# Two attention layers on one core: probabilities transposed in 64-row halves, scores in one float32 product, a staged start, and a new schedule

## The chip, the cores and the metric

The kernel runs on one core of a Trainium2 chip. The metric is the device time of one execution in microseconds (us), lower is better. The core has a matrix engine (TensorE, in the rows PE, and PEld for its weight loads), a vector engine (VectorE, DVE), a scalar engine (ScalarE, ACT), GpSimd (POOL) and a queue engine that issues the transfers (SyncE, SP). They run side by side and wait for each other through semaphores.

## The reference

The input is 16 sequences of 512 tokens of 128 features. Two blocks follow each other. Each normalises its input `xn`, then adds an attention and a feed-forward part:

```
x = x + _L0_attn_ref(xn, ...) + _L0_ffn_ref(xn, ...)      # 16 heads of 64, causal, distance penalty
xn = _layernorm(x)
x = x + _L1_attn_ref(xn, ...) + _L1_ffn_ref(xn, ...)      # 8 heads, each the difference of two softmaxes
# first attention, for each head:
sim = einsum('bhid,bhjd->bhij', q * SCALE, k) - |i - j| * slope, masked above the diagonal
out = softmax(sim) @ v
```

The second attention has 16 score maps (heads of 8 features, not causal). The feed-forward parts go from 128 to 512 features and back.

## The kernel before, in words

Every sequence is cut into 4 tiles of 128 tokens. The first attention is worked in 8 pairs of heads, the second in 16 score maps by groups of 4. There is one software pipeline: a body of 32 ticks (`TICKS`), four ticks to a pair, is written out 19 times (16 sequences and the overhang). In each body every engine has a fixed order of steps, written by hand and by tables: constants such as `LN0_AT`, `STACK_AT` or `KEY_LAG` say in which tick after a sequence's tick 0 a step stands. Numbers above 31 lie in the body of a later sequence, negative ones in that of an earlier one. So the first attention of one sequence (ticks 0 to 31 and a little more) shares a body with the second attention of an earlier one (ticks 58 to 86). Engines never reorder: what waits holds up all that stands behind it.

For one pair `p` of the first attention:

- TensorE projects q, k and v (L1304). ScalarE and VectorE together split q into `QH` and `QL`, and k into `KH` and `KL` (L795, L801, L1046, L1053): a rounded float32r part and its rest.
- `max_scores0` (L1364): for each of the four rows of 128 queries, three products `QH*KH + QL*KH + QH*KL` are summed in PSUM. The two heads stand in partitions 0 to 63 and 64 to 127, so each product is a pair of matmuls on half of the array's rows each. Row widths are 256, 256, 384 and 512 columns (at least 256).
- `row_max0` (VectorE, L1072) subtracts the distance term and takes the maximum; `exp0` (ScalarE, L827) takes the exponential and the row sums `lsum`; `invert_sums` (VectorE, L1079) takes the reciprocal of all 8 sums of a pair at once; `scale_probs` (GpSimd, L696) multiplies the 8 blocks of rows of `pq` by it, in place.
- `turn_probs` (TensorE, L1380) transposes the 20 blocks of 128x128 on and below the diagonal, in five groups that fill a PSUM tile of 512 columns each; `copy_turned` (ScalarE, L841) copies each tile to `pt`. `pv0` (L1392) multiplies by v, two heads side by side in 64 columns of the array each.

The second attention uses bf16 products for its maximum and its key scores (L1451, L1458; again two halves of rows), `pv1` (L1414; four quarters of 32 columns), and `stack`, which is SyncE's transfer of rotated queries and keys from a scratch tensor to `QS` and `KS` (L620), after `store_parts` (L610) has written them there.

All score and transpose tiles share five PSUM banks in turn (`score_order`, `SCB`): a tile may be written when the tile five places ahead of it has been read (`bank_free`). Projections and outputs share two more (`pj_order`).

Before the pipeline, 35 transfers bring in weights and tables (L568), all counted by one semaphore `s_ld`. VectorE, ScalarE and TensorE wait for all of them; then VectorE prepares the weights (21 small steps, `s_vprep`), and TensorE waits for that too.

## Time and profile before

| | us |
|---|---|
| median of 3 runs | 2792.95 (2787.28 to 2793.64) |
| the profiled execution, own time | 2788.22 |
| its span (first to last instruction) | 2786.4 |
| TensorE busy in the span | 2554.3 (92%) |
| VectorE, ScalarE, GpSimd busy | 1927.8 (69%), 1962.1 (70%), 1398.8 (50%) |
| mean granted TensorE clock, as a share of 2.4 GHz | 0.98 |

Between the profiled execution's own time and its span lie 1.8 us. Busy shares are averages over three stages: a start without matmuls, a long middle in which all sequences look alike, and an end in which only the second attention of the last sequence is left. A matmul's row shows its length with the latency; what one costs in a stream is the distance from one start to the next. The float32 matmuls stand in the trace as two matmuls each.

### The profile page before, as it was taken

The numbers are of one execution on the slowest core, as the hardware profiler recorded it, in microseconds if no ns is written. First come the engines' busy times: TensorE is split into PE (matmuls) and PEld (weight loads), VectorE is DVE, ScalarE is ACT, GpSimd is POOL, SyncE is SP. The second block draws the span as 40 slices with busy tenths as digits, with TensorE's granted clock in tenths as the row PEclk, the third lists the DMA queues.
The fourth block names the chain that finished last, engine by engine and source line by source line (L and its number), as shares of the span: only waits on it lengthen the run. The fifth ranks groups of instructions, "written<-read, shape, count | busy, mean of one in ns | idle before, by whom it ended". The sixth has DMA issues, their size and how long they took to land.

```text
span 2786.4 us, 49789 instructions
## 1 busy us (share of the span) xinstructions
PE 2554.3 (92%) x16640; PEld 1389.1 (50%) x16640; DVE 1927.8 (69%) x5381; ACT 1962.1 (70%) x4707; POOL 1398.8 (50%) x1353
## 2 busy tenths in 40 slices
PE   3788999999999999999999999999999999999867
PEld 1455555555555545555554555555455555554421
DVE  3336777677777767777776867767676776867664
ACT  2566777777777677787777868777787777778434
POOL 3556455463645546364554636456464645646211
PEclk9899999999999999999999999999999999999976
DMA  2002001020200102020010202002020200202020
GB/s 86 4 1 50 2 17 39 5 50 5 46 5 17 39 6 50 5 47 5 15 41 5 51 1 51 5 10 46 5 50 2 50 5 6 50 2 50 1 50 5
DMA packets 59822, 68.39 MB, mean 25 GB/s; under 512 B 11056, under 2 KB 55344, under 8 KB 56368
## 3 DMA queue, kind: packets, MB, share of 16 engines
q1 hardware_dynamic: 59568, 65.21, 10.3%
q8 instruction: 135, 2.21, 0.3%
q14 instruction: 119, 0.97, 0.1%
HBM read 35.04 MB, written 29.36 MB: 23 GB/s over the span
## 4 chain that ended last, share of the span: by engine, by line
PE 75%; DVE 11%; ACT 5%; issue 5%; POOL 3%; SPq 1%; DMA 0%; DVEq 0%; POOLq 0%; ACTq 0%
PE pj L1304 18%; PE sc L1364 10%; PE pj L1392 10%; PE op L1414 9%; PE sc L1380 9%; PE sc L1458 5%; PE pj L1404 4%; PE pj L1319 4%; PE sc L1451 4%; DVE pq L1072 4%; POOL pq L696 2%; DVE mx L1125 2%; ACT pt L862 2%; PE pj L1296 2%; ACT oraw L846 1%
## 5 line engine op out<-in xcount | busy, mean ns | idle before, releaser
L696 POOL TENSOR_SCALAR pq<-pq,rsum 128x128 f32<-128x128 f32 (+3 forms) x1024 | 1103.0, 1096 | 989.6 <-DVE rsum L1079 989.0
L1125 DVE TENSOR_REDUCE mx<-sc 128x1 f32<-128x512 f32 x1024 | 649.5, 681 | 213.4 <-PE sc L1458 213.2
L862 ACT ACTIVATE pt<-sc 128x512 f32<-128x512 f32 x1024 | 551.3, 601 | 213.0 <-PE sc L1451 210.8
L1072 DVE CUSTOM_DVE_ANT_0 pq<-sc,relkey 128x128 f32<-128x128 f32 (+3 forms) x1024 | 457.1, 483 | 249.2 <-PE sc L1364 242.5
L841 ACT ACTIVATE pt<-sc 128x512 f32<-128x512 f32 x640 | 381.7, 600 | 275.6 <-PE sc L1380 274.1
L827 ACT ACTIVATE pq<-pq,mx 128x128 f32<-128x128 f32 (+3 forms) x1024 | 569.0, 568 | 3.0 <-DVE mx L1072 3.0
L1380 PE MATMUL sc<-ident,pq 128*128 128x128 f32 x2560 | 395.3, 283 | 40.0 <-POOL pq L696 26.9
L1380 PEld LDWEIGHTS sc<-ident,pq 128*128 128x128 f32 x2560 | 288.9, 142 | 222.3 <-issue 130.9
L1392 PE MATMUL pj<-pt,v 128*64 128x512 f32 (+3 forms) x2048 | 303.9, 438 | 14.7 <-DVE KL L1053 13.0
L1414 PE MATMUL op<-pt,v 128*32 128x512 f32 x2048 | 282.6, 626 | 6.4 <-ACT pt L862 6.2
L1304 PE MATMUL pj<-xnT,wqkv 128*128 128x512 f32 x512 | 284.9, 640 | 0.8 <-ACT xnT L772 0.8
L1458 PE MATMUL sc<-KS,QS 48*128 48x512 bf16 x1024 | 246.0, 392 | 35.4 <-DVE mx L1072 18.1
L1364 PE MATMUL sc<-KH,QH 64*128 64x256 f32 (+2 forms) x1024 | 207.9, 399 | 22.2 <-ACT pt L862 14.1
L1392 PEld LDWEIGHTS pj<-pt,v 128*64 128x64 f32 x2048 | 141.8, 136 | 173.0 <-issue 130.6
L1451 PE MATMUL sc<-QS,KS 51*128 51x512 bf16 x1024 | 211.2, 398 | 18.1 <-ACT pt L862 7.8
L827 ACT ACTIVATION_READ_ACCUMULATOR pq<-pq,mx 128x1 f32 x1024 | 211.5, 206 | 0.0
L1364 PEld LDWEIGHTS sc<-KH,QH 64*128 64x128 f32 x1024 | 99.1, 184 | 213.4 <-issue 176.2
L1364 PE MATMUL sc<-KH,QL 64*128 64x256 f32 (+2 forms) x1024 | 168.9, 320 | 0.0
L1364 PE MATMUL sc<-KL,QH 64*128 64x256 f32 (+2 forms) x1024 | 168.8, 319 | 0.0
L1451 PEld LDWEIGHTS sc<-QS,KS 51*128 51x128 bf16 x1024 | 49.9, 93 | 213.2 <-issue 136.1
L818 ACT ACTIVATE att<-pj 128x512 f32<-128x512 f32 x128 | 76.4, 597 | 99.1 <-PE pj L1392 97.1
L1304 PE MATMUL pj<-wqkv,xnT 128*128 128x128 f32 x1024 | 145.3, 285 | 0.4 <-ACT y L789 0.4
(107 smaller groups left out, 3335.0 us busy)
## 6 DMA issues: line engine op xcount, KB each, us to landing
scr_p<-y SPq DMA_DIRECT2D x160, 128.0 KB, 2.4
QS<-scr_p SPq DMA_DIRECT2D x32, 384.0 KB, 5.8
KS<-scr_p SPq DMA_DIRECT2D x32, 384.0 KB, 8.8
x_in<-in_L_attn_x SPq DMA_DIRECT2D x16, 256.0 KB, 2.9
scr_p<-tanh SPq DMA_DIRECT2D x32, 128.0 KB, 2.4
out_x<-xres SPq DMA_DIRECT2D x16, 256.0 KB, 2.3
QS<-nrow SPq DMA_DIRECT2D x192, 4.0 KB
wqkv<-in_L_attn_w_qkv SPq DMA_DIRECT2D x1, 1536.0 KB, 8.4
```

The lines of the kernel that those rows point to most:

```text
L696: pool.tensor_scalar(rows, rows, rsum[:, p % NROWS, c:c + 1], None, ALU.mult).then_inc(s_scl, 1)
L827: act.activation(rows, rows, ACT.Exp, scale=-1.0, bias=mx0[:, p % NROWS, c:c + 1], accum_out=lsum[:, p % NROWS, c:c + 1]).then_inc(s_exp0, 1)
L841: act.activation(pt[:, base:base + T], sc[tile_bank("tr0", m)][:, :], ACT.Copy).then_inc(s_ev, 1)
L862: act.activation(pt1[:, GS * (m % 2) + 2 * j + h, :], sc[tile_bank("st1", 2 * n + h)][:, :], ACT.Exp, scale=float(DS) ** -0.25).then_inc(s ...
L1072: dve.tensor_tensor_reduce(out=pq[:, at:at + width], in0=sc[tile_bank("mx0", m)][:, left:left + width], in1=relkey[:, T - width:T], scale= ...
L1125: dve.reduce_max(mx1[:, g % 2, at:at + 1], sc[tile_bank("mx1", 2 * t + h)][:, :], AXIS.X).then_inc(s_mxd1, 1)
L1304: last = pe.matmul(t[:, c * k:c * (k + 1)], w(k), x(k), start=True, stop=True)
L1364: last = pe.matmul(sc[tile_bank("mx0", m + j)][:, left:left + width], x[r, b, P * row:P * (row + 1)], y_[r, b, 0:width], start=c == 0, sto ...
L1380: last = pe.transpose(t[:, to:to + P], pq[:, at:at + P], ident[:, :])
L1392: last = pe.matmul(t[DH * j:DH * (j + 1), P * k:T], v0[:, p % NBUF, k, DH * j:DH * (j + 1)], pt[:, base:base + WIDTH[k]], start=k == 0, st ...
L1414: last = pe.matmul(op[32 * j:32 * (j + 1), :], v1[:, k, (GS * g + j) // 2, :], pt1[:, GS * (k % 2) + j, :], start=k == 0, stop=k == NT - 1)
L1458: pe.matmul(sc[tile_bank("mx1", 2 * t + h)][:, :], QS[r, slot, P * q:P * (q + 1)], KS[r, slot, :], start=True, stop=True).then_inc(s_mxf1, 1)
```

## The change

It has five parts.

1. `turn_probs`: each block is transposed as two halves of 64 rows (`h`), which go to two PSUM tiles, in three groups (8, 8 and 4 blocks) instead of five. The copy of `copy_turned` puts the halves side by side again: six copies per pair, four of 512 and two of 256 columns.
2. `max_scores0`: one float32 product of `Q0` and `K0` instead of the three float32r ones. The rows are 128, 256, 384 and 512 columns wide. ScalarE copies q, VectorE copies k; the splitting steps are gone.
3. `invert_sums` and `scale_probs` work in four steps `q` of two sums each; the first two steps stand one pair earlier than before.
4. The loads come in three groups with a semaphore each; the first x is the first transfer of all. What prepares weights stands in ticks 1, 10 and 14 of the first body, and each first user waits for its group only.
5. Schedule: other ticks, `KEY_LAG` 14 instead of 13, another order of the steps in each tick.

```diff
-TURNED = (((0, 0),), ((1, 0),), ((0, 1), (0, 3)), ((1, 1), (1, 3)), ((0, 2), (1, 2)))
+TURNED = (((0, 0), (1, 0)), ((0, 1), (0, 3), (1, 1), (1, 3)), ((0, 2), (1, 2)))
-STACK_AT = (54, 57)
+STACK_AT = (47, 50)
-KEY_LAG = 13
+KEY_LAG = 14
@@ sync
-                for dst, src in loads:
-                    sp.dma_start(dst, src).then_inc(s_ld, 16)
+                sp.dma_start(x_in[:, :, :], x_v[0]).then_inc(s_x, 16)
+                for n in range(3):
+                    for dst, src in loads[n]:
+                        sp.dma_start(dst, src).then_inc(s_ld[n], 16)
@@ vector
-            def split_q(i, p):
-            def split_k(i, p):
+            def copy_k(i, p):
+
+                b, u = pj_use(i, f"k{p}")
+                dve.wait_ge(s_pjf[b], u)
+                dve.tensor_copy(K0[:, p % NQ, :], pj[b][:, :]).then_inc(s_pje[b], 1)
-                dve.wait_ge(s_exp0, i.upto(L0N, 8 * p + 8))
-                dve.reciprocal(rsum[:, p % NROWS, :], lsum[:, p % NROWS, :]).then_inc(s_rc, 1)
+                dve.wait_ge(s_exp0, i.upto(L0N, 8 * p + 2 * q + 2))
+                dve.reciprocal(rsum[:, p % NROWS, 2 * q:2 * q + 2], lsum[:, p % NROWS, 2 * q:2 * q + 2]).then_inc(s_rc, 1)
@@ tensor
-            pe.wait_ge(s_ld, NLOAD)
-            pe.wait_ge(s_pset, N_PSET)
-            pe.wait_ge(s_vprep, N_VPREP)
-            pe.wait_ge(s_aprep, N_APREP)
+            pe.wait_ge(s_ld[0], NLOAD[0])
-                    width = max(P * (row + 1), 2 * P)
-                    for c, (x, y_) in enumerate(((QH, KH), (QL, KH), (QH, KL))):
-                        for j in range(2):
+                    width = P * (row + 1)
+                    for j in range(2):
+                        last = pe.matmul(sc[tile_bank("mx0", m + j)][:, left:left + width], Q0[r, b, P * row:P * (row + 1)],
+                                         K0[r, b, 0:width], start=True, stop=True)
-                        last = pe.transpose(t[:, to:to + P], pq[:, at:at + P], ident[:, :])
+                    for h in range(2):
+                        r = slice(HALF * h, HALF * (h + 1))
+                        last = pe.transpose(sc[tile_bank("tr0", m + h)][:, HALF * n:HALF * (n + 1)], pq[r, at:at + P], ident[r, r])
@@ scalar, copy_turned
-                act.activation(pt[:, base:base + T], sc[tile_bank("tr0", m)][:, :], ACT.Copy).then_inc(s_ev, 1)
+                act.activation(to[:, :, h, :], sc[tile_bank("tr0", m)][:, 0:cols].rearrange("p (n c) -> p n c", c=HALF),
+                               ACT.Copy).then_inc(s_ev, 1)
```

TensorE, in the middle of the program, the last tick of one pair and the first of the next, before (`ident,pq` are the transposes, `KH`/`QH` and the like the scores, `QS,KS` the second attention, `xnT` projections):

```order
L1380 MATMUL sc<-ident,pq 128x128 x4
L1451 MATMUL sc<-QS,KS 128x512 x2
L1380 MATMUL sc<-ident,pq 128x128 x4
L1304 MATMUL pj<-xnT,wqkv 128x512
L1380 MATMUL sc<-ident,pq 128x128 x4
L1451 MATMUL sc<-QS,KS 128x512 x2
L1304 MATMUL pj<-xnT,wqkv 128x512
L1364 MATMUL sc<-KH,QH 128x256 x2
L1364 MATMUL sc<-KH,QL 128x256 x2
L1364 MATMUL sc<-KL,QH 128x256 x2
```

The same place of the changed program:

```order
L1492 MATMUL sc<-KS,QS 128x512 x2
L1411 MATMUL sc<-ident,pq 128x64 x16
L1448 MATMUL op<-pt,v 32x512 x4
L1485 MATMUL sc<-QS,KS 128x512 x2
L1492 MATMUL sc<-KS,QS 128x512 x2
L1332 MATMUL pj<-xnT,wqkv 128x512
L1485 MATMUL sc<-QS,KS 128x512 x2
L1492 MATMUL sc<-KS,QS 128x512 x2
L1332 MATMUL pj<-xnT,wqkv 128x512
L1394 MATMUL sc<-K,Q 128x128 x2
L1394 MATMUL sc<-K,Q 128x256 x2
L1411 MATMUL sc<-ident,pq 128x64 x24
```

The transposes stand in two runs of 16 and 24 halves per pair instead of five groups of 4, and next to other matmuls that use half of the array's rows. Over one whole body (the rows from one sequence to the next) TensorE changes between whole array, row halves, column halves and column quarters 138 times before and 123 times after.

GpSimd, in the middle of the program, before (`rsum` rows scale the probabilities, the others are small norms):

```order
L696 TENSOR_SCALAR pq<-pq,rsum 128x128
L696 TENSOR_SCALAR pq<-pq,rsum 128x256
L696 TENSOR_SCALAR pq<-pq,rsum 128x128
L696 TENSOR_SCALAR pq<-pq,rsum 128x256
L668 TENSOR_SCALAR veps<-mv 128x4
L670 TENSOR_TENSOR rstd<-veps,minus_half 128x4
L696 TENSOR_SCALAR pq<-pq,rsum 128x384 x2
L696 TENSOR_SCALAR pq<-pq,rsum 128x512 x2
```

After:

```order
L713 TENSOR_SCALAR pq<-pq,rsum 128x384 x2
L681 TENSOR_SCALAR veps<-mv 128x4
L683 TENSOR_TENSOR rstd<-veps,minus_half 128x4
L713 TENSOR_SCALAR pq<-pq,rsum 128x512 x2
L713 TENSOR_SCALAR pq<-pq,rsum 128x128
L713 TENSOR_SCALAR pq<-pq,rsum 128x256
L721 TENSOR_SCALAR mse<-ms 128x8
L723 TENSOR_TENSOR rms<-mse,minus_half 128x8
```

The rows are the same, but each step of two now waits only for its own two sums, and the small row blocks of the next pair follow the large ones of this pair.

SyncE, the transfers of one sequence in the middle of the program, before:

```order
L610 DMA scr_p<-y 16x8x512 x5
L610 DMA scr_p<-tanh 16x8x512
L610 DMA scr_p<-y 16x8x512 x5
L610 DMA scr_p<-tanh 16x8x512
L620 DMA QS<-scr_p 48x4096 x2
L620 DMA KS<-scr_p 48x4096 x2
L595 DMA out_x<-xres 128x4x128
```

After:

```order
L620 DMA scr_p<-y 16x8x512 x5
L620 DMA scr_p<-tanh 16x8x512
L632 DMA QS<-scr_p 48x4096 x2
L620 DMA scr_p<-y 16x8x512 x5
L620 DMA scr_p<-tanh 16x8x512
L632 DMA KS<-scr_p 48x4096 x2
L605 DMA out_x<-xres 128x4x128
```

The query stack, which waits until the key scores of the sequence before are all done, now stands in front of the stores of the key parts.

## Rows read from the trace of the kernel before

**Rows 1.** Windows: us, busy PE, PEld, DVE, ACT, POOL (x), clock, DMA, GB/s

```profile
50.00:152.50 102.50, 76.74 (x469) 48.63 (x469) 42.82 (x161) 63.10 (x169) 56.88 (x54) 0.91 0.01 4
...
1426.80:1590.00 163.20, 156.62 (x1042) 85.85 (x1041) 120.09 (x336) 122.22 (x294) 86.87 (x84) 1.00 0.11 24
2549.30:2786.40 237.10, 181.28 (x966) 73.55 (x964) 137.39 (x309) 110.97 (x229) 45.65 (x46) 0.81 0.09 20
```

**Rows 2.** Waits of PE, 500 to 2300 us: total us, times, longest

```profile
PE pj L1392 <- DVE KL L1053: 8.4, 12, 0.7
PE pj L1304 <- DVE KL L1053: 7.1, 11, 0.9
```

**Rows 3.** Waits of PE, 50 to 200 us

```profile
PE sc L1380 <- POOL pq L696: 22.5, 6, 5.1
```

**Rows 4.** Timeline of PE: start us, length us, instructions (transposes, then a projection)

```profile
1406.06 1.04 PE L1380 MATMUL sc<-ident,pq 128*128 128x128 f32 x8
1406.93 1.02 PE L1304 MATMUL pj<-xnT,wqkv 128*128 128x512 f32 x2
```

**Rows 5.** Groups by form: PE weight loads and one score matmul (mean ns last before the second bar)

```profile
L1380 PEld LDWEIGHTS sc<-ident,pq 128*128 128x128 f32 x2560 | 288.9, 142 | 222.3 <-issue 130.9 <-POOL pq L696 31.3 <-ACT pt L841 19.6
...
L1392 PEld LDWEIGHTS pj<-pt,v 128*64 128x64 f32 x2048 | 141.8, 136 | 173.0 <-issue 130.6 <-ACT pt L841 16.8
...
L1304 PEld LDWEIGHTS pj<-wqkv,xnT 128*128 128x128 f32 x1024 | 124.1, 191 | 24.1 <-issue 18.6 <-ACT y L789 4.8 <-ACT xnT L772 0.3
...
L1364 PE MATMUL sc<-KH,QL 64*128 64x256 f32 x512 | 73.9, 278 | 0.0
```

**Rows 6.** Timeline of PE: float32r scores of rows 0 and 1, and of row 3

```profile
1403.72 0.51 PE L1364 MATMUL sc<-KH,QH 64*128 64x512 f32 x2
...
1404.62 1.16 PE L1304 MATMUL pj<-w_l,xnT 128*128 128x128 f32 x8
...
1409.33 0.38 PE L1364 MATMUL sc<-KH,QH 64*128 64x256 f32 x2
1409.52 0.31 PE L1364 MATMUL sc<-KH,QL 64*128 64x256 f32 x2
...
1410.00 0.31 PE L1364 MATMUL sc<-KL,QH 64*128 64x256 f32 x2
1410.24 0.66 PE L1380 MATMUL sc<-ident,pq 128*128 128x128 f32 x4
```

**Rows 7.** Timeline of PE: transposes, values by two heads, scores of row 2

```profile
1413.33 0.60 PE L1380 MATMUL sc<-ident,pq 128*128 128x128 f32 x4
1413.86 2.37 PE L1392 MATMUL pj<-pt,v 128*64 128x512 f32 x16
1416.17 1.13 PE L1304 MATMUL pj<-xnT,w 128*128 128x512 f32 x2
...
1417.66 0.44 PE L1364 MATMUL sc<-KH,QH 64*128 64x384 f32 x2
...
1418.29 0.40 PE L1458 MATMUL sc<-KS,QS 48*128 48x512 bf16 x2
```

**Rows 8.** Groups by form: the splitting steps and the copy of a turned tile

```profile
L841 ACT ACTIVATE pt<-sc 128x512 f32<-128x512 f32 x640 | 381.7, 600 | 275.6 <-PE sc L1380 274.1
...
L1046 DVE SCALAR_TENSOR_TENSOR QL<-pj,qscale,QH 128x512 fp32r<-128x512 f32 x128 | 94.8, 740 | 50.3 <-ACT QH L795 50.3
...
L801 ACT ACTIVATE KH<-pj 128x512 fp32r<-128x512 f32 x128 | 77.0, 601 | 1.2 <-PE pj L1304 1.2
```

**Rows 9.** Timeline of PE: the first matmul of the program

```profile
39.39 1.09 PE L1296 MATMUL pj<-ident,xn 128*128 128x128 f32 x4 [39.39 <-DVE xn L1024]
```

**Rows 10.** DMA issues: KB each, median us from issue to landing

```profile
scr_p<-y SPq DMA_DIRECT2D x160, 128.0 KB, 2.4
...
KS<-scr_p SPq DMA_DIRECT2D x32, 384.0 KB, 8.8
...
wqkv<-in_L_attn_w_qkv SPq DMA_DIRECT2D x1, 1536.0 KB, 8.4
```

**Rows 11.** Timeline of SyncE: the stack of the keys is issued

```profile
1402.54 0.77 SPq L620 DMA_DIRECT2D KS<-scr_p  x2
```

More of the change, by code:

```diff
@@ L222, in pj_order @@
             order += misc
+        elif r == 1:
+            second(n, 0)
             order.append(("pv", *pair_at(s, 3)))
-        elif r == 1:
+            order += misc
+            second(n, 1)
+        elif r == 2:
+            second(n, 0)
+            order.append(("v", *pair_at(s, -1)))
+            order += misc
+            second(n, 1)
+        else:
             second(n, 0)
@@ L259, in turned @@
         p, ago = pair_at(s, lag)
-        order.append(("tr0", ago, 5 * p + g))
+        order.extend(("tr0", ago, 6 * p + 2 * g + h) for h in range(2))
     for n in range(TICKS):
@@ L307, in ago, with first @@
         return Seq(self.lo - d, self.j)
+    def first(self):
+        return self.j is None and self.lo == 0
     def live(self):
@@ L574, in load_x @@
             def load_x(i):
[L576 to L577 removed]
+                if i.first():
                     return
@@ L730, in body @@
                     s, r = divmod(n, 4)
+                    if b.first() and n == 0:
+                        clear()
                     if r == 0:
@@ L749, in body @@
                             scale_probs(i, p, 3)
+                    elif r == 2:
+                        p, i = b.pair(s, 0)
+                        if i is not None:
+                            scale_probs(i, p, 0)
                         small(b, n)
+                    else:
+                        small(b, n)
+                        p, i = b.pair(s, 0)
+                        if i is not None:
+                            scale_probs(i, p, 1)
             pipeline(pool, body)
@@ L909, in body @@
                     s, r = divmod(n, 4)
+                    if b.first():
+                        prepare(n)
                     if r == 0:
+                        p, i = b.pair(s, -1)
+                        if i is not None:
+                            copy_q(i, p)
                         second_attention(b, n, 0)
```

468 lines of the change are left out of this document (227 added, 241 removed).

## The prediction

> **What bounds the kernel now.** I looked at windows first. One sequence of the middle, from the first projection of its head pairs to that of the next, takes 163.2 us; TensorE is busy for 156.6 of it, ScalarE for 122.2, VectorE for 120.1, GpSimd for 86.9, all at the full clock (granted 1.00, the level of 2.4 GHz) [rows 1]. Thirteen such periods lie between 285.6 and 2405.3 us, 163.05 us each. So three quarters of the program is TensorE's stream, and what it spends there counts thirteen times. The waits of TensorE in the middle are small: the two largest that the change touches are for the last part of the split keys, 8.4 and 7.1 us over 1800 us, or eleven sequences [rows 2]. The start is another matter: the first matmul begins at 39.4 us [rows 9], and in the first pairs TensorE is busy for 76.7 of 102.5 us [rows 1], with 22.5 us of waits for GpSimd's scaling of the probabilities [rows 3]. The end, 237 us with 181 us of TensorE work, holds the second attention of the last sequence alone [rows 1].
>
> **Transposes.** Eight transposes of 128x128 start at 1406.06, the next step at 1406.93: 0.109 us each [rows 4], 20 per pair, 2.18 us. A half has 64 columns to stream instead of 128, and the two halves use different rows of the array, as the two heads of the scores do now. From the streaming alone a pair of halves would cost 0.055 us. Two other bounds are near. The weights (128 columns) must come in: a load of 64 columns lasts 136 ns, of 128 columns 191, so 0.86 ns per column on about 81 ns of latency; the transposes' own loads last 142 ns [rows 5], so about 61 ns without the latency. And two instructions of each kind must be issued: two score matmuls of 0.278 us [rows 5] cover 0.31 us together [rows 6], so the second starts 0.03 us after the first, and two such steps make 0.06 to 0.07. I take 0.066. From above the nearest row is the float32r pair, 0.12 us per pair of 256 columns [rows 6]; that is the bound if it is the pair and not the columns that costs. Sum: 8 pairs x 20 x (0.066 - 0.109) = **-6.9 us per sequence**; upper end +1.8.
>
> **Scores.** Before: rows 0 and 1 take 0.91 us (1409.33 to 1410.24), row 3 0.90 (1403.72 to 1404.62) [rows 6], row 2 0.63 (1417.66 to 1418.29) [rows 7]; 2.44 us. After, each head streams 128 + 256 + 384 + 512 columns in float32. That is exactly what the values step does: sixteen matmuls, two heads side by side, 1413.86 to 1416.17, 2.31 us [rows 7]. It divides columns of the array and not rows, but float32r rows go side by side as well [rows 6]. With two more entries of about 0.17 us (three groups instead of one; their drain and first load, below) it is 2.65: **+0.2 us per pair, +1.6 per sequence**. If float32 halves did not run together it would be twice the streaming, +2.1 us more per pair.
>
> **Changes of the array's division.** Four transposes from 1413.33 need 0.44, yet the values step begins 0.53 later [rows 7]; between whole-array steps nothing is lost (1406.93 above is 8 x 0.109) [rows 4]. After the scores, the next transposes start 0.24 after a last pair that needs 0.12 [rows 6]. So a change costs 0.10 us, and 0.05 to 0.11 more where the first weights can't be loaded ahead. The order has 138 changes per sequence before and 123 after: 15 x 0.15 = **-2.3 us**. The Trainium skill (TensorEngine Tiling, Key Properties) says that changing the tiling mode drains the engine; these rows agree, 0.10 us each.
>
> **Projections and copies.** K is ready after one copy instead of a ScalarE step and a VectorE step. The waits for it are (8.4 + 7.1) / 11 = **-1.4 us per sequence** [rows 2]. ScalarE loses a step of 0.60 us and gains one copy: six instead of five, two of them half as wide, about +0.2 us, from copies of 0.60 [rows 8]. VectorE loses 0.74 [rows 8] and one like it, gains a copy of about 0.6 and three more reciprocals of some 0.2 us. Both engines end a little lighter than 122 and 120 us per sequence, against 155 of TensorE; if TensorE did not cover them, these edits would still be gains.
>
> **Waits that come.** A faster TensorE meets the readers of its five PSUM banks earlier, and now writes four banks of transposes in a row, which ScalarE empties in 2 x 0.6 + 2 x 0.4 = 2.0 us while TensorE has values steps to do. I put **+1.0 us per sequence** on this, from nothing up to 5. Sum for the middle: -6.9 + 1.6 - 2.3 - 1.4 + 1.0 = -8.0, so 155 us per sequence, x 13 = **-104 us**.
>
> **The start.** Before, everything waits for all 35 transfers and then for the preparation. After, x is first, and TensorE needs eight transfers more; the largest of them lands 8.4 us after its issue [rows 10]. Issues take about 0.4 us each (two in 0.77) [rows 11], so it goes out third, at about 1.7 us, and the group is there at 10 to 12 us, and the norms of x, which need only the first transfer, fit under it. First matmul at about 12 instead of 39.4 [rows 9]: **-27 us**, of which I keep it all, since the preparation for tick 1 (about 3 us of VectorE) moves into a stage that has room.
>
> **The first pairs.** GpSimd starts when all eight sums are inverted and TensorE waits 22.5 us for it [rows 3]. After, half of the blocks are scaled before the last exponential, and I expect most of this to go, some 17 us, plus the cheaper transposes of 15 pairs, 8 us: **-25 us**. **The end:** the last sequence's eight pairs keep the same gain, **-7 us**; the 237 us behind them have neither transposes of this kind nor such scores, 0.
>
> **Sum:** 2788.2 - 104 - 27 - 25 - 7 = 2625 for a profiled execution; its own time was 4.7 us under the median of the three runs, so **2630 us**.
>
> **The rivals.**
> *Halves as dear as wholes.* A pair of halves costs 0.12 us, as a float32r pair does [rows 6], from issue or weight loads. Then the middle has +1.8 instead of -6.9 and TensorE is no faster, so no new waits come: about 0 per sequence, and the start and first pairs remain (-27 and -18): 2748 us. For it: no row shows a pair under 0.11 us. Against: 191 versus 142 ns of the loads, and the 0.03 us step. The Trainium skill (TensorE: Matmul & The Clock Gate, LDWEIGHTS) gives a load as columns / 1.2 ns whatever the number of rows, 107 ns here; by that rule the halves save nothing, and the same page (Wait, 56 ns, not 53.3 ns?) gives 62 ns per matmul if the instructions are decoded in software, 124 for a pair.
> *New waits.* The five banks, or the stack. The key stack is issued at 1402.5 [rows 11] and lands 8.8 us later [rows 10], 1411.3; the first score of the new sequence starts at 1418.3 [rows 7], 7 us of slack. After, the key parts are stored only behind the query stack: six issues of 0.4 us and more and a landing of 2.4 us [rows 10] come in between, 3 to 5 us in all, and the sequence is 8 us shorter on the way; 2 to 4 us are left. If either costs 4 us per sequence more: 2630 + 13 x 4 = 2682.
> *Float32 halves one after another (the other side).* If the two heads' float32 matmuls don't share the array, the scores take 2.1 us more per pair, 17 us per sequence: 2630 + 16 x 17 = 2900 us. It decides from 10 us per sequence on. For it: no row has float32 on row halves. Against: the values step has its sixteen matmuls in 2.31 us [rows 7], which is the time of eight.
> *The start doesn't gain.* Were the first group as late as the whole, 27 us would be missing, 2657; inside the range.
>
> **How the numbers follow.** Forecast 0.57; halves as dear 0.16; new waits 0.19; one after another 0.08. 2630 is the first. Its own range is 2590 to 2665. The range 2580 to 2750 takes in the second and third and leaves out the fourth. A measurement here tells 0.3% (8 us) from no change. Faster: the first three except 0.03 of the second, where waits would add to it, 0.89; within 0.3% 0.03; slower 0.08.
>
> **What would show it.** The distance from one pair of half transposes to the next (0.066); the length of a middle period (155); scores of row 3 at about 0.43 us per float32 pass of both heads; the first matmul at 12 us; the waits for GpSimd in the first 150 us under 6; TensorE's waits for ScalarE's copies and for `QS`, `KS`. I would be wrong if pairs of halves stand 0.11 us or more apart, if the second head's matmuls start when the first head's end, or if TensorE's idle share in a middle period rises above the 4% of now by more than 2%.

## The result, and the profile after

The changed kernel takes 2723.15 us (median of 4 runs, 2718.66 to 2727.31), the kernel before 2793.3 beside it (2787.28 to 2796.29): ratio 0.9751, 95% interval 0.9726 to 0.9776. It is faster by 70 us, where 163 were forecast. The time is inside the range, the sign is right, and the size is not: more than half of the gain is missing. (The two profiled executions show less, 60.9 us between their spans: the one before ran 5 us under its median, this one 4 us over its own.) Where the gain is missing, the windows tell. The changed kernel's, with the columns of [rows 1] (the first two sequences, one of the middle, and the stretch behind the last projections):

```profile
16.60:121.90 105.30, 84.32 (x537) 45.69 (x537) 47.15 (x196) 62.09 (x173) 59.63 (x58) 0.89 0.09 27
121.90:241.20 119.30, 107.28 (x825) 62.22 (x823) 64.27 (x247) 83.26 (x223) 80.95 (x77) 0.99 0.13 30
1377.40:1539.70 162.30, 150.93 (x1138) 75.81 (x1136) 116.51 (x353) 118.18 (x295) 87.78 (x84) 1.00 0.10 24
2496.50:2725.50 229.00, 176.57 (x1022) 69.54 (x1021) 138.25 (x315) 109.82 (x232) 44.20 (x44) 0.85 0.09 22
```

I cut both programs at the same step, ScalarE's copy of the first q of a sequence, and compared the pieces (us):

| piece | before | after | difference | forecast |
|---|---|---|---|---|
| up to the first copy of q | 43.4 | 16.6 | -26.8 | -27 |
| sequences 0 and 1 | 109.2 + 133.1 | 105.3 + 119.3 | -17.7 | -25 |
| 13 sequences of the middle | 13 x 163.05 | 13 x 162.34 | -9.3 | -104 |
| last sequence and end | 381.1 | 373.9 | -7.2 | -7 |
| span | 2786.4 | 2725.5 | -60.9 | -163 |

The start came out as forecast, and the first pairs fell 7 us short. The end agrees in number only. Cut once more, at the last copy of q, its first part holds all but the tail of the last sequence's eight pairs, before and after:

```profile
2405.30:2549.30 144.00, 139.08 (x940) 75.83 (x939) 103.58 (x281) 106.86 (x260) 72.74 (x70) 1.00 0.08 19
```

```profile
2351.60:2496.50 144.90, 134.62 (x1023) 67.31 (x1022) 101.27 (x298) 103.37 (x260) 76.78 (x73) 1.00 0.08 18
```

They gained nothing (144.0, then 144.9), and from there to the last transposes it is 54.9, then 55.8 us. The 8 us came in the stretch behind them, where none had been forecast: 237.1 us at a granted clock of 0.81 [rows 1], 229.0 at 0.85. Most of them lie between the last transposes and the last output projection, before and after:

```profile
2604.20:2641.60 37.40, 31.65 (x197) 12.99 (x199) 24.05 (x49) 19.21 (x38) 1.86 (x2) 0.91 0.01 2
```

```profile
2552.30:2582.40 30.10, 26.64 (x182) 10.15 (x178) 20.15 (x40) 16.93 (x35) 1.86 (x2) 1.00 0.01 2
```

Both the order (15 matmuls fewer fall into it) and the clock differ there, and no run parts the two. The length of the whole stretch goes with the clock in kernels of the changed order too: 234.0 us at 0.82 in e11, 225.0 at 0.87 in e3, 223.2 at 0.88 in e7.

The middle missed most: a period is 0.7 us shorter and not 8. Yet TensorE does have less to do in it, 150.9 us of 162.3 where it had 156.6 of 163.2 [rows 1]. Its idle part rose from 6.6 to 11.4 us (4% to 7%). So the work went, and idle time came in its place.

The work went as forecast. In the timeline of TensorE (start us, length us), the float32 scores of row 3 with the key scores behind them, and a run of twelve pairs of halves:

```profile
1406.32 1.13 PE L1394 MATMUL sc<-K,Q 64*128 64x512 f32 x4
1407.28 0.38 PE L1485 MATMUL sc<-QS,KS 51*128 51x512 bf16 x2
...
1418.63 0.97 PE L1411 MATMUL sc<-ident,pq 64*128 64x64 f32 x24
```

The twelve pairs start between 1418.631 and 1419.369: the last ones follow each other every 0.0625 us, and the two of a pair 3 to 4 ns apart (7 to 11 ns in the run of sixteen below). Of row 3, the first pass of both heads starts at 1406.32, the second at 1406.85, and the key score at 1407.28: the heads share the array in float32 too.

What came is in TensorE's waits over eleven sequences (403.5 to 2188.9 us; total us, times, longest):

```profile
PE sc L1411 <- DVE mx L1095: 38.1, 77, 1.0
PE sc L1492 <- DVE mx L1095: 15.8, 52, 0.5
PE sc L1394 <- ACT pt L885: 8.9, 22, 0.6
PE sc L1492 <- ACT pt L863: 8.1, 22, 0.4
```

L1411 is a transpose, L1095 VectorE's pass over a score tile that takes the row maxima; 38.1 / 11 is 3.5 us per sequence, in seven waits of half a microsecond. The kernel before, over eleven sequences (448.8 to 2242.1 us), had 4.2 there, and nearly as much as now at the maximum scores (L1458, now L1492):

```profile
PE sc L1458 <- DVE mx L1072: 14.3, 56, 0.5
PE sc L1380 <- DVE mx L1072: 4.2, 11, 1.0
```

All listed waits together rose from 63.5 to 118.2 us, 5.0 per sequence. Those for VectorE's row maxima are 3.1 of it (19.3 to 53.9 us). The waits for K gave 1.4 back. The other 3.2 are many small ones of 0.3 to 0.8 us per sequence, most of them new, for copies and sums that empty other banks (L813, L836, L863, L1069, L1116, L1148); no run tests these.

Its waits for KL [rows 2] are gone, and none for K stands in the changed kernel's list. One of the seven, in the changed kernel's timeline of all engines:

```profile
1396.14 0.93 PE L1394 MATMUL sc<-K,Q 64*128 64x128 f32 x8
...
1396.90 0.66 PE L1411 MATMUL sc<-ident,pq 64*128 64x64 f32 x16
1397.21 0.29 DVE L1095 CUSTOM_DVE_ANT_0 pq<-sc,relkey 128x128 f32<-128x128 f32 x1 [0.73 <-PE sc L1394]
...
1397.42 0.42 DVE L1095 CUSTOM_DVE_ANT_0 pq<-sc,relkey 128x256 f32<-128x256 f32 x1
...
1397.77 0.69 DVE L1076 COPY K<-pj 128x512 f32<-128x512 f32 x1
...
1398.00 0.46 PE L1411 MATMUL sc<-ident,pq 64*128 64x64 f32 x8 [0.44 <-DVE mx L1095]
```

TensorE writes the two score tiles of rows 0 and 1, then sixteen half transposes into two more banks, then wants two banks for the last eight. (One score tile belongs to each of the two heads.) With five banks in rotation the second of these is the bank of the first score tile, five tiles back. VectorE starts when the scores are done, reads the tile twice and is through at 1397.85. Sixteen halves take TensorE only half a microsecond, and it stands until 1398.00. It is VectorE that waited first (0.73 us for the scores), so no engine is overloaded here: it is a round trip with too little work beside it. (A round trip: TensorE writes a tile, VectorE reads it, and only then may TensorE write its bank again.)

### The profile page after: what moved, and what is told of

Read it like the earlier page. It is cut to its first block, busy times and chain, and to the rows that moved or that the text cites. A ratio compares the mean times of both kernels' runs of the same rounds, so it can differ in the third digit from the quotient of the medians.

```text
span 2725.5 us, 52475 instructions
## 1 busy us (share of the span) xinstructions
PE 2468.1 (91%) x18176; PEld 1232.3 (45%) x18176; DVE 1869.4 (69%) x5637; ACT 1896.9 (70%) x4707; POOL 1411.5 (52%) x1353
## 4 chain that ended last, share of the span: by engine, by line
PE 65%; DVE 14%; ACT 9%; issue 3%; DMA 0%; SPq 0%; POOLq 0%; DVEq 0%; ACTq 0%; POOL 0%
PE pj L1332 16%; PE sc L1394 10%; PE pj L1424 9%; PE op L1448 8%; PE sc L1492 5%; DVE pq L1095 5%; PE pj L1350 4%; PE pj L1438 4%; ACT pt L885 4%; PE sc L1411 4%; PE sc L1485 3%; DVE mx L1148 2%; PE pj L1324 2%; ACT pt L863 1%; ACT pq L845 1%
## 5 line engine op out<-in xcount | busy, mean ns | idle before, releaser
L1148 DVE TENSOR_REDUCE mx<-sc 128x1 f32<-128x512 f32 x1024 | 653.3, 684 | 334.3 <-PE sc L1492 331.3
L885 ACT ACTIVATE pt<-sc 128x512 f32<-128x512 f32 x1024 | 558.4, 608 | 220.2 <-PE sc L1485 219.7
L1095 DVE CUSTOM_DVE_ANT_0 pq<-sc,relkey 128x128 f32<-128x128 f32 (+3 forms) x1024 | 459.0, 486 | 315.5 <-PE sc L1394 308.3
L863 ACT ACTIVATE pt<-sc 128x512 f32<-128x512 f32 (+1 forms) x768 | 353.8, 530 | 186.9 <-PE sc L1411 185.9
L1394 PE MATMUL sc<-K,Q 64*128 64x128 f32 (+3 forms) x2048 | 383.0, 471 | 25.0 <-ACT pt L885 11.2
L1411 PE MATMUL sc<-ident,pq 64*128 64x64 f32 x5120 | 233.6, 228 | 69.0 <-DVE mx L1095 58.4
L1492 PE MATMUL sc<-KS,QS 48*128 48x512 bf16 x1024 | 243.7, 387 | 47.5 <-DVE mx L1095 20.4
L1411 PEld LDWEIGHTS sc<-ident,pq 64*128 64x128 f32 x5120 | 201.0, 140 | 177.4 <-issue 134.2
L1394 PEld LDWEIGHTS sc<-K,Q 64*128 64x128 f32 x2048 | 147.0, 187 | 252.3 <-issue 158.2
L1492 PEld LDWEIGHTS sc<-KS,QS 48*128 48x128 bf16 x1024 | 60.8, 94 | 196.3 <-DVE mx L1095 64.7
L1332 PEld LDWEIGHTS pj<-wqkv,xnT 128*128 128x128 f32 x1024 | 125.8, 193 | 39.7 <-issue 25.7
L811 ACT ACTIVATE tanh<-pj,b1h 128x512 f32<-128x512 f32 x128 | 88.3, 690 | 75.4 <-PE pj L1332 70.4
```

The source lines that it names most:

```text
L863: act.activation(to[:, :, h, :], sc[tile_bank("tr0", m)][:, 0:cols].rearrange("p (n c) -> p n c", c=HALF), ACT.Copy).then_inc(s_ev, 1)
L885: act.activation(pt1[:, GS * (m % 2) + 2 * j + h, :], sc[tile_bank("st1", 2 * n + h)][:, :], ACT.Exp, scale=float(DS) ** -0.25).then_inc(s ...
L1095: dve.tensor_tensor_reduce(out=pq[:, at:at + width], in0=sc[tile_bank("mx0", m)][:, left:left + width], in1=relkey[:, T - width:T], scale= ...
L1148: dve.reduce_max(mx1[:, g % 2, at:at + 1], sc[tile_bank("mx1", 2 * t + h)][:, :], AXIS.X).then_inc(s_mxd1, 1)
L1332: last = pe.matmul(t[:, c * k:c * (k + 1)], w(k), x(k), start=True, stop=True)
L1394: last = pe.matmul(sc[tile_bank("mx0", m + j)][:, left:left + width], Q0[r, b, P * row:P * (row + 1)], K0[r, b, 0:width], start=True, stop ...
```

## The experiments

The first theory (A): the middle is bound by such round trips. Work taken from TensorE beside one turns into waiting, and comes back as time only in part. Its rivals: (B) TensorE's work is what bounds, so the halves' gain was eaten by something that costs work; (C) VectorE's and ScalarE's work as a whole sets the period; and theories on single terms. All ratios are to the kernel before, measured on the same chip.

**e1: whole blocks in the changed order.** Banks and order as changed; each bank gets whole blocks, and ScalarE's copies, as many and as long (0.60 and 0.40 us), write them without the interleaving. (A line `...` in a cut of code stands for lines left out.)

```diff
+                half = len(blocks) // 2
...
-                    for h in range(2):
-                        r = slice(HALF * h, HALF * (h + 1))
-                        last = pe.transpose(sc[tile_bank("tr0", m + h)][:, HALF * n:HALF * (n + 1)], pq[r, at:at + P], ident[r, r])
...
+                    h, c = divmod(n, half)
+                    last = pe.transpose(sc[tile_bank("tr0", m + h)][:, P * c:P * (c + 1)], pq[:, at:at + P], ident[:, :])
```

> The changed kernel, but each block is transposed whole (one matmul of 128 columns instead of two halves of 64); same groups, tiles, copies and order. In the trace of the changed kernel a pair of halves takes 0.0625 us, a whole block took 0.109, so this adds 160 x 0.047 = 7.4 us of TensorE work per sequence. Theory A (the transposes' gain is real but was turned into waits for PSUM banks, above all the 0.6 us between the 16 and the 8 transposes of a tick, which ends when VectorE has read the scores): the added work partly fills those waits, a period of 162.3 grows to 164 to 167, in all +30 to +75 us, near 2775. Theory B (TensorE's work is the bound, and the lost time is somewhere else): +7.4 us per period, +118 us, near 2840. Theory C (the halves gain nothing at all): 2723.

Measured: 2752.81 us, ratio 0.9859 (0.9844 to 0.9873); period 164.6. In one period (columns as above):

```profile
401.00:565.50 164.50, 156.32 (x977) 80.39 (x976) 116.31 (x352) 117.98 (x295) 87.98 (x84) 1.00 0.10 24
```

The waits of the transposes for VectorE, in 403.5 to 2188.9 us, fell from 38.1 us to

```profile
PE sc L1411 <- DVE mx L1095: 6.8, 22, 0.3
```

TensorE has 5.4 us more to do than with halves and the period is 2.2 us longer; its idle part falls from 11.4 to 8.2. So 7.4 us of transposes by start-to-start distances (160 pairs of halves, 0.109 less 0.0625) are worth 2.2 us. Theory B (2840) falls; A had put the time too high as well (2775).

**e2: one pass for the scores.** Q and K as float32r, one product per tile, rows 256 columns wide at least (so the scores are coarser): a cut of TensorE's work in another place.

```diff
-        Q0 = sb("Q0", [P, NQ, T])
-        K0 = sb("K0", [P, NQ, T])
+        Q0 = sb("Q0", [P, NQ, T], F32R)
+        K0 = sb("K0", [P, NQ, T], F32R)
...
-                    width = P * (row + 1)
-                    left = P if row == 1 else 0
+                    width = max(P * (row + 1), 2 * P)
+                    left = 2 * P if row == 1 else 0
```

> The changed kernel with q and k rounded to float32r and their product taken in one pass (rows of at least 256 columns); the rounding error of the scores stays in, so the output is coarser. TensorE work falls by about 1.5 us per pair, 12 us per sequence (4 passes of 1280 columns against one pass of 1408). Theory B, TensorE's work is the bound: a period of about 150, some 190 us less in all, near 2535. Theory A, waits for banks and for the row maxima are as much of the bound as work: the scores are ready earlier too, so row maxima move forward with them, and half to two thirds of the 12 us come through: a period of 154 to 156, near 2610. If the period stays within 2 us of 162.3, TensorE's work in the scores is not on the path at all.

Measured: 2645.63 us, 0.9471 (0.9457 to 0.9485); period 157.15, in which about 5 us came back of the 12 that had been put on the cut. That is less than either forecast (B 2535, A 2610 with a period of 154 to 156). Part of it is the clock, which had stood at 1.00 in the middle of the changed kernel and does not here. Two sequences:

```profile
394.10:552.90 158.80, 143.74 (x1074) 73.85 (x1073) 116.58 (x352) 117.57 (x296) 88.49 (x84) 0.98 0.10 25
1180.50:1336.30 155.80, 140.99 (x1075) 71.74 (x1074) 116.49 (x352) 117.62 (x296) 88.56 (x84) 1.00 0.11 25
```

At 1.00 TensorE is busy for 9.9 us less than in the changed kernel, and the period is 6.5 us shorter. This is inside A's range: two thirds of the busy time came back, half of the 12. The waits for L1095 grew to 46.0 us at the transposes and 34.7 at the maximum scores (in 403.5 to 2188.9 us).

**e3: one group of loads.** x first as changed, all other transfers in one group that everything waits for.

```diff
+        loads = [loads[0] + loads[1] + loads[2]]
+        s_ld = [s_ld[0]] * 3
+        NLOAD = [16 * len(loads[0])] * 3
```

> The changed kernel, but all 35 loads are counted by one semaphore again and every first user waits for all of them (x is still the first transfer; what prepares weights stays in the first body). It undoes the staged start alone. The last load landed near 27 us before, the first group lands near 10 us now: the first projection should come about 16 us later, and the whole 14 to 18 us, near 2739. If the start's gain were only that the preparation left the path, the time would move by less than 5 us.

Measured: 2739.57 us, 0.9809 (0.9789 to 0.983). The first copy of q is at 34.1 us instead of 16.6, the period stays at 162.4: of the 26.8 us, the groups are worth 17.5 and x first with the later preparation the rest.

**e4: the second run of transposes later.** On TensorE alone, behind the small transposes, the feed-forward steps and a values step of its tick; no bank changes its place in the rotation.

```diff
-                        p, i = b.pair(s, 2)
-                        if i is not None:
-                            turn_probs(i, p, 2)
                         second_turns(b, n, 0)
                         second_turns(b, n, 1)
                         others(b, n)
                         second_values(b, n, 1)
+                        p, i = b.pair(s, 2)
+                        if i is not None:
+                            turn_probs(i, p, 2)
```

> The changed kernel, but the second run of transposes (4 blocks, two tiles) in the first tick of a pair stands behind the other steps and the values step of that tick instead of right behind the first run. No tile or bank changes its place in the turn order, only TensorE's order. Theory A says that 0.6 us per pair of waiting between the two runs (4.9 us per sequence) is time in which that other work can be done: where there is some (perhaps half of the pairs) the wait goes, 2 to 3 us per sequence, 35 us in all, near 2688. Theory B: no change, 2723. A loss would mean that ScalarE's copies of these tiles, now later, hold the next tick.

Measured: 2704.12 us, 0.9689 (0.9673 to 0.9706), 19 us faster than the changed kernel, and their intervals don't meet. Period 161.3, and sequences 0 and 1 7.7 us shorter (they scatter by a few us from kernel to kernel, below). The waits in 403.5 to 2188.9 us:

```profile
PE sc L1492 <- DVE mx L1095: 22.9, 65, 0.6
PE sc L1411 <- DVE mx L1095: 15.0, 45, 0.4
...
PE pj L1424 <- DVE y L1116: 8.8, 11, 0.8
...
PE pj L1332 <- DVE K L1076: 5.5, 11, 0.5
```

The transposes wait 23 us less, the three others here 18 us more and three further ones 11 less. Of these 17 us, 11 x 1.1 = 12 come back.

**e5, e6: VectorE's order.** In e5 the row maxima of the second score tile stand directly behind those of the first, ahead of the norms and of the copy of K; in e6 with the edit of e4 too.

```diff
                             row_max0(i, p, 0)
+                            row_max0(i, p, 1)
                         norms(b, n)
                         p, i = b.pair(s, -1)
                         if i is not None:
                             copy_k(i, p)
-                        p, i = b.pair(s, 0)
-                        if i is not None:
-                            row_max0(i, p, 1)
```

> The changed kernel with one change of VectorE's order: in the first tick of a pair the second pair of row maxima (row 2 of the scores; rows 0 and 1 are the first) follows directly on the first, ahead of the normalization steps and of the copy of the next pair's K (the copy takes about 0.66 us). Theory A, that the second run of half transposes waits about 0.6 us eight times a sequence because VectorE reads its bank late, behind the copy of K: most of the 38.1 us that TensorE waits at the transposes for row maxima in eleven sequences goes, the period falls from 162.3 to 158.5 to 160 us, time 2680 to 2700. Theory B, that TensorE waits there for something that merely comes late with the whole of VectorE's and ScalarE's work: the wait moves to another line, period 162 to 163, time 2718 to 2728.

Measured: 2730.43 us, 0.9769 (0.9751 to 0.9788), period 162.7; the waits of the transposes, in the same stretch:

```profile
PE sc L1409 <- DVE mx L1095: 40.2, 77, 1.2
```

Nothing was cured, though the length of the wait (put at 0.6; 0.5 in the rows) and of the copy of K (0.69) had looked alike. The tile that the edit moves ahead holds the second head's rows 0 and 1, not row 2 as the expectation has it. I had blamed the wrong tile: the copy stands behind the read that TensorE waits for, as the timeline above shows once the banks are counted: TensorE goes on with the last eight halves at 1398.00, in the middle of the copy (1397.77 to 1398.46).

> Both edits together: row maxima next to each other on VectorE, and the second run of transposes behind the other work of its tick on TensorE (alone 2704). Theory A, that the two cure the same wait: about what the better of the two gives, with at most 10 us on top, 2675 to 2700. Theory B, that the late run's gain came from other waits than VectorE's order: the two add up, or the new order only shifts the wait and the time stays at 2704.

Measured: 2718.59 us, 0.9737 (0.9724 to 0.9751), period 162.2: 14 us worse than e4 alone. The copy of K is now what is late; e4 had 5.5 us of this wait of a projection:

```profile
PE pj L1330 <- DVE K L1076: 18.6, 22, 1.2
```

**e7: sums inverted and blocks scaled at once,** in the second tick of the next pair (VectorE and GpSimd).

```diff
...
-                            invert_sums(i, p, 3)
+                            for q in range(4):
+                                invert_sums(i, p, q)
...
```

> The changed kernel with the row sums of a pair inverted and the blocks scaled all in the second tick of the next pair, as they stood nearly in the kernel before, in place of four steps. Theory A, that the four steps help where few pairs are in flight and change nothing in the middle: the first two sequences give back some 5 to 10 us of the 17.7 that they gained, the period stays within 0.5 us of 162.3, time 2728 to 2735. Theory B, that GpSimd's scaling in four steps keeps the middle going too: period 163 to 165, time 2740 to 2765. Theory C, that the extra small instructions on VectorE cost the middle something: period 161 to 162, time 2710 to 2720.

Measured: 2747.58 us, 0.9844 (0.983 to 0.9857). The period is unchanged (162.3), sequences 0 and 1 take 126.8 + 129.6 us, 31.8 more than in the changed kernel, and the end is 6 us shorter, at a granted clock of 0.88 in its last stretch where the changed kernel had 0.85. In 50 to 200 us:

```profile
PE sc L1395 <- POOL pq L713: 26.0, 7, 5.7
```

The changed kernel has 6.8 us of this there, the one before 22.5 [rows 3]. So the program is 24 us slower, all from the start, more than twice what A gave to the steps. Not all of the 31.8 us is waiting. The two sequences:

```profile
16.10:142.80 126.70, 90.33 (x537) 49.36 (x537) 47.77 (x194) 62.43 (x172) 60.26 (x56) 0.86 0.08 22
142.80:272.50 129.70, 111.43 (x826) 64.22 (x824) 65.60 (x247) 83.46 (x222) 80.79 (x76) 0.95 0.12 27
```

The same matmuls keep TensorE busy for 201.8 us at 0.86 and 0.95, and for 191.6 at 0.89 and 0.99 in the changed kernel. These 10 us go with the lower clock.

**e8: float32 scores alone, in the kernel before.** One product of copied Q and K instead of three of split ones.

```diff
-                    for c, (x, y_) in enumerate(((QH, KH), (QL, KH), (QH, KL))):
+                    for c, (x, y_) in enumerate(((Q0, K0),)):
```

> The kernel before with one part of the change alone: scores of the first attention from one float32 product, Q and K copied once each (by ScalarE and by VectorE), no splitting; transposes in whole blocks, order and loads as before. By the terms on record, +1.6 us of TensorE work and -1.4 us of waits for KL a sequence: 2795, no change. By the traces of the two kernels, where the scores' columns rose from 14.9 to 17.7 us a sequence (+2.8) and the waits go: +1.4 a sequence, 2815. Theory C, that ScalarE and VectorE, each freed of some 5 us of copies a sequence, come earlier with everything else: 2760 to 2785.

Measured: 2804.34 us against 2791.16, 1.0042 (1.003 to 1.0055): slower. The period is 164.35 (+1.3), and in it:

```profile
449.40:613.70 164.30, 158.08 (x978) 80.93 (x977) 114.84 (x328) 118.54 (x287) 86.91 (x84) 1.00 0.11 24
```

TensorE's work is 1.5 us more, as forecast (+1.6). The waits for K did not go (403.5 to 2188.9 us; there had been 8.4 and 7.1 us for KL [rows 2]):

```profile
PE pj L1384 <- DVE K L1046: 11.5, 22, 0.9
...
PE pj L1296 <- DVE K L1046: 7.1, 11, 0.6
```

TensorE's two waiting steps, the values of the pair and a projection, read no K: they want the bank of K's projection, which VectorE's step is the last to read. That step stands where it stood, behind the row maxima, which would be why one step instead of two frees the bank no sooner. And 5 us of work less on VectorE and 4 less on ScalarE gave nothing; theory C falls here.

**e9: one more read of the first score tile,** 256 columns into a buffer that nobody reads, before the read that frees the tile.

```diff
+                    if c == 1:
+                        dve.tensor_tensor_reduce(out=twice[:, 0:width], in0=sc[tile_bank("mx0", m)][:, left:left + width],
+                                                 in1=relkey[:, T - width:T], scale=-SLOPES[2 * p + j], scalar=-MASKED,
+                                                 op0=ALU.add, op1=ALU.min, accum_out=twice_mx[:, 0:1])
```

> The changed kernel with one more read by VectorE of the score tile of rows 0 and 1 (128x256, into a buffer that nobody reads; 0.35 us, eight a sequence), just before the read that gives the tile free. Theory A, that the second run of half transposes waits for exactly this tile (with five banks in rotation it takes the bank of the first score tile of its tick, and VectorE's two reads of it end after the first run): the period rises by nearly eight times 0.35 us, +2.3 to +2.9 us, time 2753 to 2762. Theory B, that the wait at the transposes stands for something that is late anyway: period within 0.5 us of 162.3, time 2718 to 2730.

Measured: 2759.47 us, 0.9874 (0.9861 to 0.9888); period 164.8, +2.4 for eight reads, 0.30 us of each 0.35. The waits of the transposes (402.5 to 2215.1 us):

```profile
PE sc L1417 <- DVE mx L1101: 61.6, 77, 1.4
```

38.1 has become 61.6, 2.1 us per sequence. VectorE is busy for 119.2 of 164.7 us meanwhile, so it is not its load: this one read is on the path in nearly every pair. Theory A's mechanism is shown, and the tile is the right one. What it doesn't show is that the period would shrink by as much without the wait; e10 asks that.

**e10, e11: the first run of transposes ahead of the scores,** on TensorE, in the rotation and in ScalarE's copies; then no transpose wants VectorE's tile. e11 has the edit of e4 too.

```diff
+            turned(s, 2, 1)
             second(n, 0)
             tops(s, 0, 0)
-            turned(s, 2, 1)
             turned(s, 2, 2)
```

> The changed kernel with the first run of half transposes (sixteen) moved ahead of the score tiles of its tick on TensorE, and ScalarE's copies of it moved ahead of its exponentials; the second run then takes a bank that ScalarE and not VectorE gives free, and the score tile is read while other products run. Theory A, that the price is the chain score tile, VectorE's read, transposes: the 38.1 us of waits for row maxima at the transposes go below 10, the period falls to 158 to 160.5, time 2670 to 2700. Theory B, that in order issue only moves the wait to another tile of the five banks (ScalarE's copies late): period 161 to 163, time 2705 to 2730. Theory C, that exponentials and scores, half a microsecond later in their tick, delay the row maxima of the second attention: period over 163, time over 2735.

Measured: 2731.13 us, 0.9781 (0.9766 to 0.9795), period 161.7. The wait at the transposes fell from 38.1 to 3.0 us; in its place (411.6 to 2190.5 us):

```profile
PE sc L1490 <- DVE mx L1093: 21.4, 66, 0.4
PE sc L1490 <- ACT pt L863: 13.3, 44, 0.3
PE pj L1422 <- DVE y L1114: 12.0, 11, 1.1
PE pj L1422 <- DVE K L1074: 10.8, 22, 0.7
...
PE sc L1409 <- DVE mx L1093: 3.0, 11, 0.3
```

3.2 us of waits per sequence went, and the period fell by 0.6. The first two sequences took 9.1 us more, which outweighs it. That is theory B of this run (whose 2730 it misses by 1 us): the wait moves, here above all to the values step (L1422), which needs a bank that VectorE empties late. The new order moves ScalarE's and TensorE's other steps too, so the run doesn't price the one wait alone.

> As the run before, with the second run of transposes also behind the other work of its tick (which alone gave 2704). Theory A: 2660 to 2690, a little under the run before it, as the two waits are parts of one. Theory B: 2700 to 2715.

Measured: 2743.99 us, 0.9816 (0.9801 to 0.9831), period 162.3. What helped alone (e4) costs 13 us here, and both theories (2660 to 2690, 2700 to 2715) are wrong; no run says why.

**e12: float32r scores in the changed kernel.** Splits on ScalarE and VectorE and three products, all else as changed.

```diff
-                        last = pe.matmul(sc[tile_bank("mx0", m + j)][:, left:left + width], Q0[r, b, P * row:P * (row + 1)],
-                                         K0[r, b, 0:width], start=True, stop=True)
...
+                            last = pe.matmul(sc[tile_bank("mx0", m + j)][:, left:left + width], x[r, b, P * row:P * (row + 1)],
+                                             y_[r, b, 0:width], start=c == 0, stop=c == 2)
```

> The changed kernel with the scores of the first attention as before: Q and K split into a high and a low part by ScalarE and VectorE, three float32r products a tile at the old places of the splits; half transposes, order and loads as in the changed kernel. In the kernel before the float32 scores alone cost 13 us (2804 against 2791). Theory A, that they cost the same here: 2708 to 2715. Theory B, that in the changed order, with ScalarE and VectorE nearer to TensorE's path, the splits' two further instructions a pair cost more than the columns save: 2735 to 2760. Terms on record: the float32 scores are worth 0.2 to 1.2 us a sequence less work than waits, so 2720 to 2740.

Measured: 2743.27 us, 0.9817 (0.9803 to 0.983), period 163.9 although TensorE has 1.3 us less to do in it:

```profile
406.00:569.40 163.40, 149.60 (x1202) 80.10 (x1200) 122.97 (x360) 121.63 (x304) 87.89 (x84) 1.00 0.10 24
```

The waits for the row maxima (L1115) at the transposes grew from 38.1 us:

```profile
PE sc L1435 <- DVE mx L1115: 46.8, 66, 1.8
```

So the two splitting steps more per pair seem to lengthen the round trip. But 163.9 is a mean of two kinds of sequences. Some take 163.1 to 163.5 us, mostly at clock 1.00 as above, the others 164.2 to 164.4 at 0.99, such as

```profile
1388.60:1553.00 164.40, 151.22 (x1202) 80.23 (x1200) 122.83 (x360) 121.68 (x304) 87.38 (x84) 0.99 0.10 24
```

Float32 scores cost 1.3 us a sequence in the old kernel. In the new one they are worth 0.8 to 1.1 at equal clock, and 1.6 with the lower clock of this run. Their price is not a property of theirs.

## Why the prediction was wrong

Of the kernel before, e8, e1 and the changed kernel, each adds to the one ahead: float32 scores; then, all at once, the new order and banks with loads and steps; then halves.

| | period | TensorE busy | idle |
|---|---|---|---|
| before | 163.05 | 156.6 | 6.6 |
| + float32 scores (e8) | 164.35 | 158.1 | 6.2 |
| + order, banks, early steps (e1) | 164.6 | 156.3 | 8.2 |
| + halves (the changed kernel) | 162.3 | 150.9 | 11.4 |

(Busy and idle are of one period each, at clock 1.00.) The step that failed is **"Waits that come"**, +1.0 us per sequence with 5 as the upper end. Term by term:

- *Transposes*, -6.9: the pair takes 0.0625 us where 0.066 were taken, so the work is 7.4 us less. Right, and the rival "halves as dear as wholes" is false. The prediction weighed the Trainium skill (TensorE: Matmul & The Clock Gate, LDWEIGHTS), by which a load would take 107 ns whatever the rows; here each half of the rows takes a new load of 128 columns every 62.5 ns, so the trace does not agree with that for this form. Of 7.4 us, 2.2 reached the period (e1).
- *Scores*, +1.6: e8 measured +1.5 of TensorE's work and +1.3 of the period. Right. The rival "one after another" is false.
- *Changes of the array's division*, -2.3: e1 differs from e8 by order and banks, and has 1.8 us less work and 2.0 more idle. The gain may well be in the work; none of it reached the period.
- *Waits for K*, -1.4: they did go in the changed kernel, but by the order, and not by the single copy, as I had it: e8 has the copy and keeps the waits (they are for the bank and not for K). That the place of VectorE's step decides is argued from this, and from e6, where the copy stands later and 18.6 us of such waits come.
- *Waits that come*, +1.0: TensorE's idle part should have gone from 6.6 to about 6.2 by my terms (-1.4 + 1.0); it went to 11.4. That is 5.2 of the some 7 us by which the period was missed; the rest is busy time, 5.7 less where the terms gave 7.6 (busy ends of matmuls are modelled, so the split between the two is rough). The thought was there (a faster TensorE meets the readers of its five banks earlier), but I looked at ScalarE's copies, which cost 0.7 us per sequence (8.1 us for L863 in the list above), and put a guess on the rest. The tile with the largest wait is VectorE's, 3.1 of the 5.0 us by which the listed waits rose: scores at 1396.14, VectorE's first read at 1397.21, free at 1397.85. Counting five banks on in the new order would have named it before any run: between the scores and the transposes that reuse their bank stand sixteen halves, 0.5 us of work from 1396.90 on, and the bank is free 0.95 us after that. In the order before, eight whole blocks (0.87) and a tile of the second attention stood between, and the reuser was the next such tile.
- *The start*, -27: -26.8 (e3 gives the groups' part as 16). *The end*, -7: -7.2, and this is luck. The last sequence's pairs, on which all of it was put, gained nothing (144.0 to 144.9); the stretch behind them, put at 0, gave 8.1, at a granted clock of 0.85 instead of 0.81.
- *First pairs*, -25: -17.7, by profiled executions that differ by a few us here (sequences 0 and 1 took 219 to 227 us in e1, e2, e3, e5 and e9, whose edits touch them little). The scaling in steps alone is worth 32 us of these sequences (e7), 10 of them by the clock; 17 had been put on it. What else the change did there cost 14 (256.4 in e7 against 242.3 before), part of it again at a lower clock (0.86 and 0.95 in e7; before, 0.92 in sequence 0 and 0.98 in sequence 1). Two errors in part cancelled. A third was in the sum: 8 us stood for the transposes of 15 pairs, where the term's own 0.86 us per pair gives 13.

The rival "new waits" gave 2682 from 4 us per sequence. The idle time beyond the forecast is 5.2 us, by its rule 2630 + 13 x 5.2 = 2698, and the busy time that did not go adds 13 x 1.9 = 25, which makes 2723. That this is the measured time to the microsecond is luck: the first pairs' 7 us and the end stand beside it, and so does the scatter of the profiled executions. Its mechanism, five banks and a late reader, is the largest single part, and I gave it 0.19 and too small a price. The other new waits are small and spread over many steps. The signal named as fatal, an idle share up by more than 2% of the period, is what happened (4% to 7%). Its other half, the stack of keys, was no wait: it lands in 5.6 us, and TensorE's list has no wait for it.

What stays open: which order would give the saved 7.4 us back. e4 is the best kernel here, 2704.12 us, ahead of both; its idle part is still 10 us. e5, e6, e10 and e11 show that mending one wait shows the next. That these are all of one kind, round trips and not load, is shown for one tile (e9) and only argued for the others. Why the clock fell in the middle of e2 and e12 is open too.

## What to carry to other kernels

Where engines pass a few banks around in a fixed order, price a cut of work by what stands between the write of each tile and the reuse of its bank: count the banks on in the new order, put the reader's latency (start, reads) beside the work left between, and take only what is over. A saving next to such a round trip may return a third or a half of itself (2.2 of 7.4 us in e1, 6.5 of 12 in e2 at equal clock). Mending the one wait need not pay either, where others stand close behind it (e10: 3.2 us of waits gone, 0.6 back). Compare stretches at the same granted clock, and compare them piece by piece: a sum that agrees can hide two pieces that don't (the end, here). A term read in one schedule (the float32 scores: +1.3, then about -1) holds for that schedule only, so measure an edit in the kernel in which it is to live. Where few stages are in flight, at the start, finer steps (e7, 24 us of the program's time) and early loads (e3, 16 us) pay in full.

## What the runs showed of the hardware

- Two half transposes (64 rows by 128 columns in, 64 columns streamed), on the two halves of the rows, start 3 to 11 ns apart, and pairs follow every 62.5 ns, each with two weight loads whose records last 135 to 140 ns. Whole blocks take 109 ns [rows 4]. The Trainium skill (TensorE: Matmul & The Clock Gate, Wait — 56ns, not 53.3ns?) has about 62 ns per matmul where they are decoded in software. Here two matmuls fit into that time, so that bound is not at work; how they are decoded no run shows.
- Float32 products of two heads with 64 rows each run at the same time; a pass of 512 columns for both takes 0.53 and 0.43 us (1406.32, 1406.85, 1407.28).
- VectorE's read of a 128x256 score tile costs 0.35 us in its queue (1397.42 to 1397.77); e9 puts 0.30 of it on TensorE's path. Between the (modelled) end of the scores, 1397.07, and VectorE's first read lie 0.14 us.
- The stretch behind the last projections takes 229.0 us at a granted clock of 0.85 in the changed kernel, 225.0 at 0.87 in e3, which differs only in its loads. A middle sequence of e2 takes 158.8 us at 0.98 and 155.8 at 1.00.
- ScalarE's copy of a 128x512 tile that is written in pieces of 64 columns takes 0.60 us (596 ns), as long as the plain copy of e1 (595 ns).
